# Routed experts of a graph network: expert offsets loaded four at a time, and the second group's ranks one part later

## What is computed

```python
logits = tokens @ router_w.T
probs = softmax(logits)
rw, re = top_k(probs, 2)                      # two of eight experts per node
rw = rw / max(rw.sum(-1), 1e-12)
combine = zeros((N, 8)).at[arange(N)[:, None], re].set(rw)
out = tokens
for e in range(8):
    h = gelu(tokens @ w1[e] + b1[e])          # 256 x 256
    y = h @ w2[e] + b2[e]                     # 256 x 256
    out = out + combine[:, e:e + 1] * y
x = x + out
```

## Time and profile before

| | us |
|---|---|
| three runs | 1976.6, 1979.16, 1989.29 |
| their median | 1979.16 |
| the profiled execution | 1980.88 |
| its span in the trace | 1979.1 |
| TensorE busy in the span | 1756.2 (89%) |
| VectorE busy | 909.4 (46%) |
| ScalarE busy | 567.9 (29%) |
| GpSimd busy | 153.4 (8%) |

### The profile page before, as it was taken

How to read it: one execution, slowest core, us unless ns; L and a number is a source line. 1 busy time by engine, 2 the same in 40 slices (tenths; PEclk the granted TensorE clock), 3 DMA queues, 4 the chain that set the end, 5 groups by cost and what they waited for, 6 DMA issues and landing times.

```text
span 1979.1 us, 30746 instructions
## 1 busy us (share of the span) xinstructions
PE 1756.2 (89%) x10296; PEld 1392.2 (70%) x10300; DVE 909.4 (46%) x1479; ACT 567.9 (29%) x868; POOL 153.4 (8%) x165
## 2 busy tenths in 40 slices
PE   1579999888888899999999999799999999998991
PEld 1268888888876677777777777666567777676871
DVE  5879999999882011102032233421312233246343
ACT  0013467788884210001011111242400000014540
POOL 3000000000000100000000000000000000151354
PEclk8789999999999899999999999899999999999996
DMA  2040334445458544445434334100045433442554
GB/s 89 19 150 16 126 139 176 190 191 220 195 229 343 145 133 133 142 139 151 153 115 128 116 120 129 50 1 0 0 144 195 133 116 116 132 156 94 157 154 139
DMA packets 125902, 260.95 MB, mean 132 GB/s; under 512 B 14924, under 2 KB 67302, under 8 KB 125466
## 3 DMA queue, kind: packets, MB, share of 16 engines
q1 hardware_dynamic: 108154, 240.30, 35.6%
q0 software_dynamic: 5568, 12.82, 2.1%
q10 hardware_dynamic: 12128, 7.16, 1.3%
HBM read 160.44 MB, written 108.04 MB: 136 GB/s over the span
## 4 chain that ended last, share of the span: by engine, by line
issue 56%; PE 25%; DVE 8%; ACT 4%; ACTq 2%; DMA 2%; POOL 1%; SPq 1%; DVEq 1%; POOLq 0%
PE ps L1789 10%; PE ps L1855 3%; PE ps L1790 3%; DVE act_c L1251 3%; PE ps L2066 2%; PE ps L2050 2%; ACT wide L755 2%; ACTq L800 2%; ACT ps L704 2%; PE ps L1760 1%; PE ps L1872 1%; PE ps L2058 1%; POOL act_c L1065 1%; PE ps L2042 1%; DMA wide<-weight_matrix 1%
## 5 line engine op out<-in xcount | busy, mean ns | idle before, releaser
L1855 PE MATMUL ps<-wide 128*128 128x320 f32 (+1 forms) x2000 | 534.8, 428 | 2.9 <-DVE pair_tab L1491 2.9
L1789 PE MATMUL ps<-early,act_c 128*128 128x200 bf16 x3552 | 439.0, 253 | 69.5 <-ACT ps L704 31.5
L1855 PEld LDWEIGHTS ps<-wide 128*128 128x128 f32 x2000 | 379.9, 191 | 144.6 <-DVE pair_tab L1491 3.0
L1789 PEld LDWEIGHTS ps<-early,act_c 128*128 128x128 bf16 x3552 | 327.7, 98 | 89.7 <-issue 88.1
L1790 PE MATMUL ps<-early,act_c 128*128 128x208 bf16 x1184 | 302.3, 255 | 0.0
L1251 DVE TENSOR_TENSOR act_c<-act_c,pair_tab 128x3072 bf16<-128x3072 bf16 x148 | 257.0, 1756 | 33.0 <-PE ps L1790 32.4
L1855 PE MATMUL ps<-wide,act_a 128*128 128x320 f32 (+1 forms) x1000 | 265.8, 428 | 1.8 <-ACTq L787 1.8
L1855 PEld LDWEIGHTS ps<-wide,act_a 128*128 128x128 f32 x1000 | 190.9, 191 | 74.3 <-issue 3.0
L755 ACT COPY wide<-ps 128x832 f32<-128x832 f32 x200 | 169.9, 849 | 131.1 <-PE ps L1790 128.0
L1355 DVE TENSOR_TENSOR wide<-ps,rows 128x1280 f32<-128x1280 f32 x10 | 14.9, 1492 | 412.1 <-PE ps L1872 412.1
L704 ACT ACTIVATE ps<-wide 128x832 f32 (+1 forms) x200 | 173.4, 868 | 33.9 <-ACT wide L755 32.5
(11 more groups left out here) (232 smaller groups left out, 1368.4 us busy)
## 6 DMA issues: line engine op xcount, KB each, us to landing
wide<-weight_matrix SPq DMA_DIRECT2D x90, 800.0 KB, 4.5
wide<-count_matrix SPq DMA_DIRECT2D x45, 800.0 KB, 4.5
weight_matrix<-wide SPq DMA_DIRECT2D x60, 480.0 KB, 2.5
count_matrix<-wide SPq DMA_DIRECT2D x60, 480.0 KB, 2.6
weight_matrix<-wide SPq DMA_DIRECT2D x20, 560.0 KB, 2.7
count_matrix<-wide SPq DMA_DIRECT2D x20, 560.0 KB, 2.7
expert_replies<-wide SPq DMA_DIRECT2D x63, 128.0 KB, 1.7
wide<-weight_matrix SPq DMA_DIRECT2D x20, 400.0 KB, 3.6
```

Source lines behind the costliest of these rows:

```text
L1789: nc.tensor.matmul(weights, hot_parts[:, slot % MASK_BATCHES, part, two, :, k], hot_key[:, mask_slot, mask_two, 0:WCOLS, k], start=False, ...
L1855: i = nc.tensor.matmul(ps[:, 2 * sub + h, 0:n], features[:, q * QUADS + t, h * P:(h + 1) * P], moving, start=q == 0 and t == 0, stop=q == ...
```

## The change

`experts_at` now loads at most four offsets at a time (`FEW`), and the loads are spread over the parts. On TensorE `part` takes the whole dictionary of offsets and, when a new four is due from the next part on, loads it after `make_hidden` and before `turn_hidden` (`load_ahead`). On VectorE each four is loaded just before the hidden bias of its first part. The loads that reach two parts back at the head of a loop or of the written-out end are a load of two on VectorE and part of the first four on TensorE.

So TensorE has, in place of four loads: one of four before the stage, then loads inside parts 3, 7, 11 (four each) and 15 (two); in each turn of the loop one of four at the head and one inside the parts 1, 5, 9, 13 and 17 of the turn; and one of three at the end. VectorE has loads of four before the parts 0, 4, 8, 12 and one of two before 16; in each turn one of two and one of four at the head, and three more of four; at the end one of two and one of four at the head, two more of four and one of one.

Apart from that, `group_ranks(1)` on TensorE moves from part 12 to part 13 (`RANKED`), and on VectorE `place_experts(1)`, `place_tokens(1)` and `experts_of_parts(1)` move from 13, 14, 15 to 14, 15, 16. Nothing that is computed changes.

```diff
+FEW, RANKED = 4, 13
 VectorE:
-            expert = experts_at(0, SIDE_PARTS)
+            expert = {}
             for i in range(SIDE_PARTS):
+                if i % FEW == 0:
+                    near = range(i, min(i + FEW, SIDE_PARTS))
+                    expert.update(zip(near, experts_at(near.start, len(near))))
                 add_hidden_bias(i, i, expert[i])
...
-                if i == 13:
+                if i == RANKED + 1:
                     place_experts(1)
-                if i == 14:
+                if i == RANKED + 2:
                     place_tokens(1)
-                if i == 15:
+                if i == RANKED + 3:
                     experts_of_parts(1)
             with dve.Fori(0, 2) as turn:
-                expert = experts_at(turn * DVE_TURN + SIDE_PARTS - 2, DVE_TURN + 2)
-                for k in range(DVE_TURN):
-                    n = SIDE_PARTS + k
-                    add_hidden_bias(turn * DVE_TURN + n, n, expert[k + 2])
-                    add_reply_bias(turn * DVE_TURN + n - 2, n - 2, turn + 1, expert[k])
+                first = SIDE_PARTS - 2
+                expert = dict(zip(range(first, first + 2), experts_at(turn * DVE_TURN + first, 2)))
+                for n in range(SIDE_PARTS, SIDE_PARTS + DVE_TURN):
+                    if (n - SIDE_PARTS) % FEW == 0:
+                        expert.update(zip(range(n, n + FEW), experts_at(turn * DVE_TURN + n, FEW)))
+                    add_hidden_bias(turn * DVE_TURN + n, n, expert[n])
+                    add_reply_bias(turn * DVE_TURN + n - 2, n - 2, turn + 1, expert[n - 2])
-            expert = experts_at(DVE_END - 2, PARTS - DVE_END + 2)
+            expert = dict(zip(range(DVE_END - 2, DVE_END), experts_at(DVE_END - 2, 2)))
             for i in range(DVE_END, PARTS + 2):
                 if i < PARTS:
-                    add_hidden_bias(i, i, expert[i - DVE_END + 2])
+                    if (i - DVE_END) % FEW == 0:
+                        near = range(i, min(i + FEW, PARTS))
+                        expert.update(zip(near, experts_at(near.start, len(near))))
+                    add_hidden_bias(i, i, expert[i])
...
 TensorE:
-            def part(i, n, loads, expert, expert_before):
+            def part(i, n, loads, expert, load_ahead=None):
                 if n + 1 < PARTS:
                     turn_routed(i + 1, n + 1, loads)
                 if n < PARTS:
-                    make_hidden(i, n, expert)
+                    make_hidden(i, n, expert[n])
+                if load_ahead is not None:
+                    expert.update(zip(load_ahead, experts_at(i - n + load_ahead.start, len(load_ahead))))
                 if 1 <= n <= PARTS:
                     turn_hidden(i - 1, n - 1)
                 if n >= 2:
-                    make_reply(i - 2, n - 2, expert_before)
+                    make_reply(i - 2, n - 2, expert[n - 2])
+            def ahead(n, first, end):
+                near = n + 1
+                return range(near, min(near + FEW, end)) if (near - first) % FEW == 0 and near < end else None
...
-            expert = experts_at(0, SIDE_PARTS)
+            expert = dict(enumerate(experts_at(0, FEW)))
...
-                if i == 12:
+                if i == RANKED:
                     group_ranks(1)
-                part(i, i, (i + 1) // XBUFS + 1, expert[i], expert[i - 2] if i >= 2 else None)
+                part(i, i, (i + 1) // XBUFS + 1, expert, ahead(i, 0, SIDE_PARTS))
...
             with pe.Fori(0, 2) as turn:
-                expert = experts_at(turn * PE_TURN + SIDE_PARTS - 2, PE_TURN + 2)
+                first = SIDE_PARTS - 2
+                expert = dict(zip(range(first, first + FEW), experts_at(turn * PE_TURN + first, FEW)))
+                for n in range(SIDE_PARTS, SIDE_PARTS + PE_TURN):
+                    part(turn * PE_TURN + n, n, turn * (PE_TURN // XBUFS) + (n + 1) // XBUFS + 1, expert, ahead(n, first, SIDE_PARTS + PE_TURN))
```

More of the change, by code:

```diff
@@ L1708, in _ @@
                     moe_weights_of(last)
-                if i == 13:
+                if i == RANKED + 1:
                     place_experts(1)
-                if i == 14:
+                if i == RANKED + 2:
                     place_tokens(1)
-                if i == 15:
+                if i == RANKED + 3:
                     experts_of_parts(1)
             with dve.Fori(0, 2) as turn:
-                expert = experts_at(turn * DVE_TURN + SIDE_PARTS - 2, DVE_TURN + 2)
-                for k in range(DVE_TURN):
-                    n = SIDE_PARTS + k
-                    add_hidden_bias(turn * DVE_TURN + n, n, expert[k + 2])
-                    add_reply_bias(turn * DVE_TURN + n - 2, n - 2, turn + 1, expert[k])
-            expert = experts_at(DVE_END - 2, PARTS - DVE_END + 2)
+                first = SIDE_PARTS - 2
[6 more added lines that the diff above has]
+            expert = dict(zip(range(DVE_END - 2, DVE_END), experts_at(DVE_END - 2, 2)))
             for i in range(DVE_END, PARTS + 2):
                 if i < PARTS:
-                    add_hidden_bias(i, i, expert[i - DVE_END + 2])
-                add_reply_bias(i - 2, i - 2, (i - 2) // YBUFS, expert[i - DVE_END])
+                    if (i - DVE_END) % FEW == 0:
+                        near = range(i, min(i + FEW, PARTS))
+                        expert.update(zip(near, experts_at(near.start, len(near))))
+                    add_hidden_bias(i, i, expert[i])
+                add_reply_bias(i - 2, i - 2, (i - 2) // YBUFS, expert[i - 2])
                 if i - DVE_END < len(GROUP_TILES[0]):
@@ L2086, in _ @@
                     side_step(2, SUPERS - 1, 3)
-                if i == 12:
+                if i == RANKED:
                     group_ranks(1)
-                part(i, i, (i + 1) // XBUFS + 1, expert[i], expert[i - 2] if i >= 2 else None)
+                part(i, i, (i + 1) // XBUFS + 1, expert, ahead(i, 0, SIDE_PARTS))
             pe.wait_ge(experts_ready, 2)
             with pe.Fori(0, 2) as turn:
-                expert = experts_at(turn * PE_TURN + SIDE_PARTS - 2, PE_TURN + 2)
[L2093 to L2096, removed]
+                first = SIDE_PARTS - 2
+                expert = dict(zip(range(first, first + FEW), experts_at(turn * PE_TURN + first, FEW)))
+                for n in range(SIDE_PARTS, SIDE_PARTS + PE_TURN):
+                    part(turn * PE_TURN + n, n, turn * (PE_TURN // XBUFS) + (n + 1) // XBUFS + 1, expert, ahead(n, first, SIDE_PARTS + PE_TURN))
+            near = range(PE_END - 2, min(PE_END - 2 + FEW, PARTS))
+            expert = dict(zip(near, experts_at(near.start, len(near))))
             for i in range(PE_END, PARTS + 2):
-                part(i, i, (i + 1) // XBUFS + 1, expert[i - PE_END + 2] if i < PARTS else None, expert[i - PE_END])
+                part(i, i, (i + 1) // XBUFS + 1, expert, ahead(i, PE_END - 2, PARTS))
 _INS = ['x', 'src', 'dst', 'edge_weight', 'L0_gnn_W1', 'L0_gnn_b1', 'L0_gnn_g1', 'L0_gnn_be1', 'L0_gnn_W2', 'L0_gnn_b2',
```

## The result

The changed kernel took 1974.2 us (median of 13 runs) where the kernel before took 1980.7 us in the same comparison: ratio 0.9970, 95% interval 0.9957 to 0.9984. That is 6.5 us less, where no change was forecast; the interval leaves no change out, and rival 1 had said 6.6 us less.

A forecast was written before the change was run, and what follows sets the result against it. TensorE was taken to bound the routed stage, the only part the edit reaches. Gains of 2.3 us (0.85 + 1.35 + 0.1) met losses of 2.3 (1.9 + 0.4): no change, 1979.2 us, range 1970.5 to 1986.

The forecast's parts named there:

- rival 1: TensorE's second turn entry: the 3.93 us belong to the load of 24 itself, so entry costs 0; 1972.6 us; chance 0.32.
- (d): TensorE's second turn entry: 3.93 us of the 6.083 us load are the branch back's and stay; gain 1.35 us.
- (f): VectorE's turn heads: one load of 18 becomes two, of two and four, 1.6 us; gain 0.1 us each.
- (a): TensorE before the routed stage: the load of 18 becomes four, hidden before and after; 0.
- (b): TensorE's loads inside parts: 0.8 us each, hidden under a cover of 1.2 us; 0.
- (c): TensorE's first turn entry: load shrinks from 2.16 to 0.8 us, but `experts_ready` comes a part later; gain 0.85 us.
- (e): VectorE's loads inside the loop: about 0.4 us late, within slack of about 1.1 us; 0.
- (g): VectorE in the first 18 parts: loads paid at parts 4, 12 and 16 beside side work; loss 1.9 us.
- (h): VectorE among the `combine` steps: two loads lose about 0.2 us each; loss 0.4 us.
- The ranks: Ranks moved from part 12 to 13: the 2.73 us stop gives no gain, TensorE waits elsewhere; 0, bounds -0.3 and +0.3.
- Rival 3: VectorE's small loads at parts 4, 12, 16, `combine` steps and turn heads cost nearly what large ones do; 1985.8 us; chance 0.11.
- Rival 2: Second turn's entry: the stall stays but the granted clock doesn't fall; 1976.3 us; chance 0.10.

The follow-up runs named there:

- e3: e1 with TensorE's two turns loading their 24 offsets from a table of their own, the second turn's from column 24 instead of 38; median 1980.6 us against 1985.7.
- e4: e1 with TensorE's loop of two turns written out as straight code, no branch between; first transpose to end 201.2 us against 203.9.
- e9: e2 plus 36 unused TensorE register loads behind the last part, 1 to 24 registers from six columns; 24 took 1.61 us from column 20, 6.09 from 17.
- e5: e1 with only TensorE's side of the change (offsets in fours between parts); median 1978.99 us, ratio 1.0002 to the kernel before.
- e1: Kernel before, with a lower bound on the values two message-stage waits use, base for other runs; 1985.71 us, ratio 1.0030 to the kernel before.
- e2: Changed kernel with a lower bound on the values two message-stage waits use, second base; 1982.07 us, ratio 1.0011 to the kernel before.
- e6: e1 with only VectorE's side of the change (its smaller loads); first transpose to end 206.1 us against 203.9.
- e7: e1 with only the second group's ranks moved one part later, no load changed; first transpose to end 203.3 us against 203.9.
- e12: e2 plus unused TensorE loads in another order, first twelve of 24 registers from columns 24, 16, 20; two took 3.4 and 3.6 us, the other ten 1.6 to 2.2.
- e8: e2 with every load of four in the turns and end starting at a multiple of four, on both engines; 1977.49 us, ratio 0.9998 to the kernel before.
- e10: e1 with the whole offset table shifted two columns on, on both engines; first transpose to end 212.2 us against 203.9.

## Why the prediction was wrong

**Step (d) failed.** It said of the two loads of 24 that "code, table and number of values are the same both times; what differs is the branch back just ahead". What differs too is the operand `turn * PE_TURN + SIDE_PARTS - 2`, which is 16 and then 38, and 22 is no multiple of four. The 3.93 us belong to the load (rival 1): they vanish with the branch kept and the column changed (e3), and stay with the branch gone (e4). The rule on a taken branch that waits for code, cited from the Trainium skill (Runtime: NRT & Kernel Launch, Instruction fetch mechanics), does not account for the 3.93 us: the 6.1 us stand in straight code too. The forecast kept the stop and its clock, 6.6 us by its own sum; from part 40 to 45 the change gave 7.46 us where (d) gave 1.35.

The forecast held evidence against itself, named it under rival 1 and gave it 0.32: 6.08 and 2.16 us were the times of one record each, the load's own.

**The price of a small load** was no one number. 0.8 us was taken; it is 0.34 for four from a multiple of four, 0.54 for two, and 1.0 to 1.2 for four from elsewhere. The floor of about 600 ns that the Trainium skill gives (DMA: Bandwidth & Descriptors) does not hold here: one register took 0.30 us in e9. (The forecast's estimate by that floor, 0.8 us lower, left out its own (f), where it is 0.4 us more at each head.)

**(a), (b)** right: no load of TensorE made a part longer, and in the second turn 1.1 us loads stay hidden too (from part 45 to 62 e5 takes 37.02 us, e1 37.01).

**(c)** right at its place and then lost. From part 18 to part 19 the traces show 3.93 us before and 3.21 after, a gain of 0.72, and `experts_ready` costs nothing that can be seen; but from part 18 to part 24 only 0.06 of it is left, as VectorE is late at its own head: 0.65 us come back at part 20, 0.41 of them as the stop at 1828.28. Before, TensorE's 1.21 us stop hid that lateness. This is a stall that was taken out and came back one engine on.

**(e), (f)** were put at 0 and +0.1. (The sum takes the 0.1 of (f) once, though it says it of each turn.) Two loads of 0.54 and 1.2 us at each head are no shorter than one of 1.73, and at VectorE's three heads they cost 0.8 us together (e2 less e5).

**(g)** said a loss of 1.9; measured 0 (50.86 to 50.77 at part 18). Four registers cost 0.35 us there, not 0.8, and by part 12 the change has even gained 0.3 (part 12 starts at 31.60 before, 31.29 after, 31.32 in e6), which the larger waits at parts 13 and 17 (0.82 and 0.45 us) give back. **(h)** was right: it said 0.4 for two loads among the `combine` steps, and parts 56 and 60 got 0.23 and 0.30 us longer, 0.5 together. From part 62 to the end after takes 0.5 more than before, but e2 is like e1 there, so nothing was shown. **The ranks**: right, the stop of 2.73 us came back as 3.42 us at the bias of part 12, and neither e2 nor e7 shows a gain of it.

The sum: -0.1 to part 18, -0.1 to 24, +0.1 to 40, -7.5 to 45, +0.6 to 62, +0.5 to the end: -6.5 us, as measured between the medians. That rival 1's total, 6.6 us, met this so closely is luck in part: its reason for the second entry was right (7.9 said, 7.5 measured), but its total also holds a loss of 1.9 in the first 18 parts that did not come, a gain of 0.85 at the first entry that was lost again, and nothing behind the last part, where the profiles differ by 0.5.

**Rival 3** (VectorE's loads cost what large ones do) had a grain: at columns 18, 22 and on, four do cost 1.1 us, but hidden in all places but the heads and the `combine` steps. **Rival 2** did not arise, as no stop was left.

## What to carry to other kernels

When one instruction takes two times in two turns of a loop, write down every operand that depends on the turn, the address modulo small powers of two among them, before anything outside the instruction is blamed. Lay out tables that are loaded into registers so that each load begins at a multiple of four 32-bit columns, and is a multiple of four long; here turns of 22 parts spoiled it every second time. And a stall taken from the bounding engine pays only as far as the next engine was not hiding behind it: VectorE's turn head came to light as soon as TensorE no longer stopped at its own.

## What the hardware showed that was not expected

- Where nothing else slows it, a register load of 24 values takes 1.61 us or 5.7 to 6.5 us by its first column; eight 0.60 or 1.9 to 2.7; four 0.34 or 1.0 to 1.2; one, two and three showed no such rule (two of their 18 records, 1.01 and 1.15 us, stand out). Swept on one table, at all four columns modulo four on TensorE; on VectorE only multiples of four and two beyond were seen. Where in memory the tables begin was never varied, so whether the column or the address counts is open.
- Loads from good columns can still be slow for a time (3.4 to 5.1 us for 24 between 1939 and 1947 us in e9 and e12). What does it stays open, as does the 4487 ns load of L1774 in the earlier trace rows, which by its column should be fast.
- The granted clock fell to 0.50 behind the masks' stop of 2.7 or 3.4 us in five profiles (e3, e6, e7, e8, e10) and stayed at 1.00 behind the same stop in the others. The forecast took 2.73 us of idle time as safe; it is not, always.
